# Serving the requests of a two-layer graph network while its second layer still runs: rows sorted by when they are ready, the output filled early, fewer sign passes in the sort

## The chip, the cores and the metric

The kernel runs on one core of a Trainium2 chip. The metric is the device time of one execution in microseconds, lower is better. The core has five engines that run their own programs and meet at semaphores: TensorE (PE), VectorE (DVE), ScalarE (ACT), GpSimd (POOL) and SyncE (SP). SP issues the plain transfers, POOL the indirect ones (a gather or a scatter by a list of row numbers, 128 rows each). All transfers run on the core's 16 DMA engines.

## What is computed

```python
NTOKEN, NINP, NHID, NEDGE = 18750, 64, 128, 300000
def gcn_conv(x, W, b, src, dst, n):
    h = x @ W
    deg = jnp.zeros((n,), h.dtype).at[dst].add(1.0) + 1.0
    dinv = jax.lax.rsqrt(deg)
    norm = dinv[src] * dinv[dst]
    agg = jax.ops.segment_sum(h[src] * norm[:, None], dst, num_segments=n)
    return agg + h * (dinv * dinv)[:, None] + b
h = gcn_conv(emb, W1, b1, src, dst, NTOKEN)
nodes = gcn_conv(h, W2, b2, src, dst, NTOKEN)
return nodes[input.reshape(-1)].reshape(512, 200, NINP)
```

`input` holds 102,400 request numbers from 23 to 149,996. A number past the last of the 18,750 rows is clamped to the last row, so about seven in eight requests take that one row. The output is 102,400 rows of 64 float32 numbers, 26.2 MB.

## The kernel before

Both weight matrices are multiplied into one ahead, so each layer is a sum over edges of scaled rows. The program has these stages.

1. Degrees of the nodes are counted with one-hot matmuls.
2. The 300,000 edges are sorted by a bitonic network on VectorE over 128 x 2560 keys (`steps`; `exchange` writes a minimum and a maximum, lines 1287 and 1288). The first seven levels work within a row of keys. Ahead of them `sign` steps multiply all keys by plus or minus one (line 1296), so that every exchange can go upward. Between levels PE turns the keys, and VectorE uses the time for `requests(n)`, one piece of work on the requests for each turn.
3. Two layers of 466 batches each (`NB`). In a batch PE gathers source rows out of the table in SBUF (line 989), ACT copies them out of PSUM (line 830), PE adds them into destination sums (line 1054), and VectorE makes the one-hot operands (lines 1465 and 1560). What does not fit this scheme (700 lists of 128 edges a layer) is fetched by POOL, row by row, from the table in HBM into `zring`, a ring of 18 buffers (line 684), and PE adds it (lines 1020 and 1025). The order of these items is a plan written ahead (`planned`, `ITEMS`). POOL waits on `zmm` for a free buffer, so it runs up to 18 items ahead of PE.
4. When a group of rows is complete (a unit, `UNITS`: three blocks of 128 rows, or two blocks of the last 33), VectorE scales it and SP stores it (`unit_out`). In layer one it goes to `table1`, in layer two to `nodes` (line 560), and all blocks of a group finish in the order of the groups.
5. The requests. Each partition owns 800 requests. VectorE has picked those that are not the last row, eight at a time with the largest keys first (`requests`, `comp`). The key holds the request's place in its upper bits and the row in its lower bits, so they are in the order of places. After layer two POOL gathers them, a column of 128 rows at a time (line 730), and scatters them into the output (line 739). It works by `q` of ten columns behind an `If`, as many as the fullest partition needs. Ahead of the scatters `filled` is awaited: SP has written the last row over the whole output (line 610), 25 rows a piece, from `zring`.

At the end VectorE turns `comp` into the two lists of numbers (lines 1573 to 1577) in the last batch. POOL's queue there, in program order: the last ring gathers, a skipped `If` for a slow way that is taken when lists overflow (`many`), three loads of counts, the wait for all stores of `nodes`, the gathers, the wait for `filled`, the scatters, the waits for their landing.

The fetch of sorted key rows that prepares layer one works in fifteen pieces (`prep_steps`): `rank_rows(g)` and `cell_rows(g)` on POOL stand between ring gathers, and `begins(g)` on VectorE waits for the first of them (line 1363). Piece 1 is fetched after the first 18 ring gathers, and `begins(1)` stands in batch 2.

## Time and profile before

| what | value |
|---|---|
| median of three executions | 4097.41 us (4090.86 to 4101.44) |
| the profiled execution | 4114.96 us, its span 4113.1 us |
| busy: PE, DVE, ACT, POOL | 2787.5, 3019.4, 1326.7, 1867.6 us |
| degrees and set-up | 0 to 363 us |
| sort | 363 to 1040 us |
| layer one | 1070 to 2433 us |
| layer two | 2433 to 3740 us |
| gathers and scatters of the requests | 3740 to 4113 us |

A busy share is an average over stages with different limits. The chain that ended last is the better guide: it is followed back from the last instruction, at each step to what released it.

### The profile page before, as it was taken

What the parts mean: (1) busy time and instruction counts of PE and PEld (TensorE: products, weight loads), DVE (VectorE), ACT (ScalarE), POOL (GpSimd) and SP (SyncE); (2) the same over time, 40 slices, a digit from 0 to 9 for tenths busy, and PEclk for the clock granted to TensorE, in tenths of its full rate; (3) what the DMA queues carried; (4) which work ended last, traced back from release to release, by engine and by line L of the source; (5) the groups of instructions that cost most, each with busy time, mean ns of one, the idle gap of its engine ahead of it and who ended that gap; (6) DMA issues with size and microseconds to landing.
All of it is one profiled execution on the core that took longest, in us unless ns stands there. A gap on an engine that the chain in (4) does not pass through costs nothing.

```text
span 4113.1 us, 74778 instructions
## 1 busy us (share of the span) xinstructions
PE 2787.5 (68%) x27730; PEld 2494.4 (61%) x27730; DVE 3019.4 (73%) x8656; ACT 1326.7 (32%) x3124; POOL 1867.6 (45%) x1717
## 2 busy tenths in 40 slices
PE   6996434421477888888888867888888888883000
PEld 5884222211367777877877766888887888882000
DVE  9999999999577887877777866777777777773000
ACT  5774212210433333433333322333333333331000
POOL 2000000000465556666656645666666565555765
PEclk9997566655699999999999988999999999996555
DMA  3000000000223233333333342333333333336400
GB/s 75 0 0 4 19 12 16 19 4 0 64 77 83 76 78 79 86 79 79 81 81 82 83 134 69 80 84 82 85 82 81 77 82 80 78 81 252 60 24 9
DMA packets 202648, 269.00 MB, mean 65 GB/s; under 512 B 99119, under 2 KB 111704, under 8 KB 202039
## 3 DMA queue, kind: packets, MB, share of 16 engines
q1 hardware_dynamic: 147912, 185.41, 15.1%
q0 software_dynamic: 54416, 79.31, 10.3%
q8 instruction: 203, 3.33, 0.3%
q14 instruction: 117, 0.96, 0.1%
HBM read 213.38 MB, written 52.14 MB: 65 GB/s over the span
## 4 chain that ended last, share of the span: by engine, by line
PE 47%; DVE 32%; issue 6%; another core or an unknown queue 6%; POOL 5%; ACT 2%; POOLq 1%; SPq 1%; DMA 0%; DVEq 0%; ACTq 0%
PE ps L989 17%; PE ps L1054 17%; PE ps L871 8%; DVE oh L1560 7%; DVE keys L1287 6%; DVE keys L1288 6%; DVE keys L1465 4%; POOL arena L730 3%; PE ps L1020 2%; POOL out L739 2%; DVE zoh L1544 2%; PE ps L937 1%; PE ps L1025 1%; POOLq L739 1%
## 5 line engine op out<-in xcount | busy, mean ns | idle before, releaser
L684 POOL DMA_INDIRECT zring<-table,sidx x1400 | 1560.2, 1114 | 1055.2 <-PE ps L1020 533.8
L989 PE MATMUL ps<-arena,keys 128*128 128x192 bf16 x11184 | 1283.9, 253 | 271.1 <-issue 132.1
L830 ACT ACTIVATE steps_oh<-ps 128x384 bf16<-128x384 f32 x1864 | 898.7, 490 | 1723.7 <-PE ps L989 1296.2
L1054 PE MATMUL ps<-steps_oh,oh 128*128 128x192 bf16 x11172 | 1276.9, 252 | 1.9 <-issue 1.9
L989 PEld LDWEIGHTS ps<-arena,keys 128*128 128x128 bf16 x11184 | 970.5, 100 | 340.1 <-issue 205.2
L1054 PEld LDWEIGHTS ps<-steps_oh,oh 128*128 128x128 bf16 x11172 | 985.7, 100 | 12.8 <-issue 3.1
L1560 DVE TENSOR_SCALAR oh<-io_h,dl 128x384 bf16<-128x384 int16 x3724 | 960.0, 319 | 44.9 <-remote 28.0
L1465 DVE TENSOR_SCALAR keys<-keys,lanes 128x1024 bf16<-128x1024 int16 x1398 | 596.5, 480 | 16.7 <-DMA keys<-srel 10.6
L639 POOL DMA_INDIRECT arena<-line,row_i x16 | 15.8, 988 | 1030.4 <-DVEq L1351 1025.9
L1544 DVE TENSOR_SCALAR zoh<-io_h,dl 128x128 bf16<-128x128 int16 x1172 | 261.2, 263 | 301.6 <-remote 147.5
L937 PE MATMUL ps<-ident,keys 128*128 128x128 f32 x464 | 100.1, 409 | 319.8 <-DVE keys L1288 315.3
L1020 PE MATMUL ps<-zring,zoh 128*128 128x192 bf16 x1172 | 217.7, 253 | 119.3 <-DVE oh L1560 79.7
L937 PEld LDWEIGHTS ps<-ident,keys 128*128 128x128 f32 x464 | 92.5, 222 | 335.6 <-DVE keys L1288 330.7
L1287 DVE TENSOR_TENSOR keys<-keys 128x1280 f32<-128x1280 f32 (+4 forms) x233 | 278.9, 1197 | 17.6 <-ACT keys L801 9.5
L1288 DVE TENSOR_TENSOR keys<-keys 128x1280 f32<-128x1280 f32 (+4 forms) x233 | 277.4, 1190 | 0.0
L758 ACT ACTIVATE steps_oh<-colf,arena 128x128 bf16<-128x128 f32 x784 | 240.4, 389 | 78.8 <-PE ps L871 78.7
L1138 DVE TENSOR_TENSOR oh<-iorep,arena 128x1024 bf16<-128x1024 bf16 (+1 forms) x392 | 258.6, 714 | 0.4 <-DVE arena L1188 0.4
L871 PE MATMUL ps<-oh 128*128 128x147 bf16 x1568 | 231.1, 314 | 0.3 <-DVE oh L1138 0.3
L1020 PEld LDWEIGHTS ps<-zring,zoh 128*128 128x128 bf16 x1172 | 99.2, 99 | 173.5 <-DVE oh L1560 119.2
L871 PEld LDWEIGHTS ps<-oh 128*128 128x128 bf16 x1568 | 173.2, 118 | 40.7 <-DVE oh L1138 17.6
L1547 DVE TENSOR_SCALAR ooh<-io_h,dl 128x384 bf16<-128x384 int16 x228 | 71.6, 324 | 161.2 <-PE ps L1054 89.6
L739 POOL DMA_INDIRECT out<-arena,oidx x130 | 127.7, 982 | 67.9 <-issue 67.9
(249 smaller groups left out, 1615.8 us busy)
## 6 DMA issues: line engine op xcount, KB each, us to landing
keys<-srel SPq DMA_DIRECT2D x466, 256.0 KB
out<-zring SPq DMA_DIRECT2D x1, 25600.0 KB
zring<-table,sidx POOLq DMA_INDIRECT x1400
table<-arena SPq DMA_DIRECT2D x19, 384.0 KB, 2.8
table<-sgn_l SPq DMA_DIRECT2D x38, 144.0 KB
nodes<-arena SPq DMA_DIRECT2D x38, 96.0 KB
arena<-in_L_rec_edge_index SPq DMA_DIRECT2D x2, 1171.5 KB, 6.6
arena<-nodes,oidx POOLq DMA_INDIRECT x130
```

What stands on the lines that cost most here:

```text
L684: pool.indirect_dma_start(out=zring[:, i % RING, :], out_offset=None, in_=rows_of, in_offset=bass.IndirectOffsetOnAxis(ap=sidx[:, col:col ...
L830: act.activation(grow[:, j % 2, h * 2 * ROW:(h + 1) * 2 * ROW], pg[h][:, 0:2 * ROW], ACT.Copy).then_inc(evac, 1)
L871: mm = pe.matmul(bank[:, 0:BLOCKS], lane[:, t // TT, :, t % TT] if steps is None else stp[:, t, :], blk[:, t // TT, :, t % TT], start=Fals ...
L989: mm = pe.matmul(pg[t // 2][:, t % 2 * ROW:(t % 2 + 1) * ROW], s_oh[:, j // 2 % 2, k, e:e + P], xtab[:, (w * WIN + k) * ROW:(w * WIN + k + ...
L1020: pe.matmul(pz[:, 0:ROW], zoh[:, u, :], zring[:, u, :], start=False, stop=(n == (ZT if blk < ZB - 1 else ZLAST) - 1)).then_inc(zmm, 1)
L1054: mm = pe.matmul(sums(sl, k), dwin[:, j % 2, t, k * P:(k + 1) * P], grow[:, j % 2, t * ROW:(t + 1) * ROW], start=False, stop=(w == CELLS - ...
L1138: dve.tensor_tensor(o.rearrange("p (s j t) -> p s j t", s=HH // TT, t=TT), iorep[:, 0:m, :].unsqueeze(1).to_broadcast([P, HH // TT, m, TT] ...
L1287: dve.tensor_tensor(b[:, :, 0, :], a[:, :, 0, :], a[:, :, 1, :], ALU.min).then_inc(k_stage, 1)
L1288: dve.tensor_tensor(b[:, :, 1, :], a[:, :, 0, :], a[:, :, 1, :], ALU.max).then_inc(k_stage, 1)
L1465: made = dve.tensor_scalar(s_oh[:, p % 2, k, :], srow[:, p % 2, :], lanes[:, k:k + 1], None, ALU.is_equal)
L1544: dve.tensor_scalar(zoh[:, place[item], :], io_h[:, 0:P], dl[:, col:col + 1], None, ALU.is_equal)
L1560: made = dve.tensor_scalar(dwin[:, j % 2, t, :], io_h[:, off:off + SUP * P], dl[:, c:c + 1], None, ALU.is_equal)
```

## The change

**Requests.** `nodes` gets a new layout (`stores`, `slot_of`): 38 slots of 512 rows, a group's three blocks and then one of the last 33 blocks. The key now holds 32767 minus the row's place in this layout in its upper bits and the request's place in its lower ten, so `comp` begins with the rows that are stored first. `requests(1)` has sixteen operations of 128x800 where it had three. The first 60 columns (`EG` = 6 times 10) get their lists in layer one (`places`, `early_checks`). In layer two POOL gathers them between ring gathers (`early_gather`), each ten once the units before `UPTO[q]` are stored. It scatters the first 20 (`SG` = 2) the same way (`early_scatter`). After layer two the `If` of a group that is done is skipped.

**Output.** The last block of the small lists comes first in layer two (`Z_ORDER`), so the last row is known early. SP reads it into `fill` as 128 x 16 copies and writes the output in 50 pieces, one after every second pair of batches. Layer two's first small list starts at batch 12 instead of 10.

**Sort.** Six of the seven sign steps are gone. The first six levels exchange upward and downward in four instructions ("two ways"), each half as wide.

**Fetch.** `rank_rows(1, 2)` stands before the first ring gather of layer one, and piece 1 begins in batch 5.

```diff
+SLOT = 4 * P
+EG, SG = 6, 2
+GROUPS = [groups_with((q + 1) * OG - 1) for q in range(EG)]
@@ steps of the sort
-        steps = [("sign", 0, k_b, k_a, 0, ALL, 0)]
+        steps = []
...
-            if 1 < k < 8:
+            if k == 7:
                 steps.append(("sign", k - 1, cur, other, done, ALL, 0))
...
+                if k < 7:
+                    steps.append(("two ways", (1 << bit, 1 << (k - 1 - bit)), cur, other, done, ALL, 0))
+                    done, cur, other = done + 4, other, cur
+                    continue
@@ vector: the step itself
+                elif what == "two ways":
+                    stride, n = k
+                    a, b = (x.rearrange("p (g d m t s) -> p g d m t s", d=2, m=n, t=2, s=stride) for x in (src, dst))
+                    for d in range(2):
+                        low, high = a[:, :, d, :, 0, :], a[:, :, d, :, 1, :]
+                        dve.tensor_tensor(b[:, :, d, :, d, :], low, high, ALU.min).then_inc(k_stage, 1)
+                        dve.tensor_tensor(b[:, :, d, :, 1 - d, :], low, high, ALU.max).then_inc(k_stage, 1)
@@ planned
+        Z_ORDER = [list(range(ZB)), [ZB - 1] + list(range(ZB - 1))]
-            total, given, items, wait_until = len(left) + OT, 0, [], 10 * layer
+            total, given, items, wait_until = len(left) + OT, 0, [], 12 * layer
+        UPTO = [units_for(q) for q in range(EG)]
+        STORED_AT = [UNITS[1][upto - 1][2] + 10 for upto in UPTO]
+        FILL_FROM, FILL_STEP, FILLS = 16, 2, RT // FILL
+        SCATTER_AT = 2 * (FILL_FROM + FILL_STEP * FILLS) + 16
         def prep_at(g):
-            return 2 + 4 * (g - 1)
+            return 2 + 4 * (g - 1) if g > 1 else 5
@@ sync: the fill
+            def fill_part(i):
+                if i == 0:
+                    for s in EMPTY:
+                        sp.dma_start(nodes[s * SLOT + SUP * P:(s + 1) * SLOT, :], acc3[:, BLOCKS, :]).then_inc(last_in, 16)
+                    sp.wait_ge(tab1_out[LAST_UNIT % UR], rows_out(LAST_UNIT + 1, LAST_UNIT % UR))
+                    sp.dma_start(fill.rearrange("p (t f) -> p t f", f=F),
+                                 nodes[LAST_AT:LAST_AT + 1, :].unsqueeze(1).to_broadcast([P, FILL, F])).then_inc(last_in, 16)
+                else:
+                    sp.wait_ge(last_in, 16 * (len(EMPTY) + 1))
+                    sp.dma_start(rows[:, i - 1, :], fill).then_inc(filled, 16)
@@ pool: in the loop over the items of layer two
+                    for q in range(EG):
+                        first = FIRST_ITEM[1][min(STORED_AT[q], NB)] + RING
+                        for n in range(OG):
+                            between.setdefault(min(first + 3 * n, NI), []).append((early_gather, q * OG + n))
+                    for t in range(SG * OG):
+                        between.setdefault(min(FIRST_ITEM[1][SCATTER_AT] + RING + 4 * t, NI), []).append((early_scatter, t))
@@ pool: after layer two
-                    with pool.If(most > r * ROUND + q * OG):
+                    with pool.If((again if q < EG else most) > r * ROUND + q * OG):
                         for t in range(q * OG, (q + 1) * OG):
                             pool.indirect_dma_start(
...
+                for q in [*range(SG, QG), *range(SG)]:
+                    with pool.If((again if q < SG else most) > r * ROUND + q * OG):
```

How the change moves instructions, at three places. First POOL from layer two to the slow way behind it, where `zring<-table,sidx` is a ring gather and the rows behind the COMPARE_AND_BRANCH are the skipped slow way; before:

```order
L684 DMA zring<-table,sidx 128x192 x700
L691 COMPARE_AND_BRANCH
L693 DMA keys<-line 128x20x128
L694 UNCONDITIONAL_BRANCH
L694 ISA
```

and now, around the third early group (item 477 of the ring gathers) and then from the end of the fifth (item 648 on), where `arena<-nodes,eidx` is an early request gather and `out<-arena,eidx` an early scatter:

```order
L798 DMA zring<-table,sidx 128x192 x4
L759 DMA out<-arena,eidx 102400x64
L798 DMA zring<-table,sidx 128x192 x11
L750 DMA arena<-nodes,eidx 128x64
L798 DMA zring<-table,sidx 128x192 x3
L750 DMA arena<-nodes,eidx 128x64
```

```order
L750 DMA arena<-nodes,eidx 128x64
L798 DMA zring<-table,sidx 128x192 x3
L750 DMA arena<-nodes,eidx 128x64
L798 DMA zring<-table,sidx 128x192 x25
L750 DMA arena<-nodes,eidx 128x64 x10
L808 COMPARE_AND_BRANCH
```

The early groups stand from ring item 261, 348, 477, 561 and 648 of 700 on, one gather after every third item. The sixth group has no item left and stands behind all of them. The 20 scatters stand from item 390 to 466, one after every fourth.

Second the SP queue in the first part of layer two, where `keys<-srel` feeds VectorE's one-hots, before:

```order
L569 DMA keys<-srel 128x1024 x10
L560 DMA nodes<-arena 128x3x64
L569 DMA keys<-srel 128x1024 x6
L560 DMA nodes<-arena 128x3x64
L569 DMA keys<-srel 128x1024 x2
```

and now, from the first stores on:

```order
L631 DMA nodes<-arena 128x3x64
L631 DMA nodes<-arena 128x64
L652 DMA keys<-srel 128x1024 x5
L640 DMA nodes<-arena 128x64 x5
L642 DMA res<-nodes 128x16x64
L652 DMA keys<-srel 128x1024
L631 DMA nodes<-arena 128x3x64
L652 DMA keys<-srel 128x1024
L646 DMA out<-res 128x1024
L652 DMA keys<-srel 128x1024 x2
L646 DMA out<-res 128x1024
```

Five small stores, the read of the last row and then 50 output pieces have come into the queue that feeds VectorE.

Third the first levels of the sort on VectorE, before:

```order
L1296 TENSOR_TENSOR keys<-keys,sgn_t 128x2560
L1287 TENSOR_TENSOR keys<-keys 128x1280
L1288 TENSOR_TENSOR keys<-keys 128x1280
L1296 TENSOR_TENSOR keys<-keys,sgn_t 128x2560
L1287 TENSOR_TENSOR keys<-keys 128x640x2
```

and now:

```order
L1453 TENSOR_TENSOR keys<-keys 128x640
L1454 TENSOR_TENSOR keys<-keys 128x640
L1453 TENSOR_TENSOR keys<-keys 128x640
L1454 TENSOR_TENSOR keys<-keys 128x640
L1453 TENSOR_TENSOR keys<-keys 128x320x2
```

The passes over all 2560 keys have gone, and each pair of instructions has become two pairs of half the width.

## Rows read from the trace of the kernel before

**Rows 1.** The page: its span, and the chain that ended last by line
```profile
span 4113.1 us, 74778 instructions
...
PE ps L989 17%; PE ps L1054 17%; PE ps L871 8%; DVE oh L1560 7%; DVE keys L1287 6%; DVE keys L1288 6%; DVE keys L1465 4%; POOL arena L730 3%; PE ps L1020 2%; POOL out L739 2%; DVE zoh L1544 2%; PE ps L937 1%; PE ps L1025 1%; POOLq L739 1%
```

**Rows 2.** Stretches: busy PE, PEld, DVE, ACT, POOL; PEclk, DMA share, GB/s
```profile
2500.00:3740.00 1240.00, 1067.08 (x11847) 999.61 (x11847) 914.26 (x3421) 436.33 (x906) 743.19 (x672) 0.95 0.32 79
3740.00:3902.00 162.00, 0.00 (x0) 0.00 (x0) 1.82 (x1) 0.00 (x0) 122.54 (x130) 0.50 0.63 187
3902.00:4113.10 211.10, 0.00 (x0) 0.00 (x0) 0.00 (x0) 0.00 (x0) 127.80 (x131) 0.50 0.09 17
```

**Rows 3.** The order of time on POOL: last table gather, first request gather
```profile
3709.05 0.94 POOL L684 DMA_INDIRECT zring<-table,sidx  x1 [1.15 <-PE ps L1020]
3740.15 0.94 POOL L730 DMA_INDIRECT arena<-nodes,oidx  x1 [30.16 <-issue]
```

**Rows 4.** The order of time, VectorE and the SP queue, end of layer two
```profile
3731.68 0.26 SPq L563 DMA_DIRECT2D nodes<-arena  x1
...
3734.15 1.03 DVE L1577 TENSOR_TENSOR dl<-keys 128x840 int32<-128x840 f32 x1
...
3736.90 0.38 SPq L560 DMA_DIRECT2D nodes<-arena  x1
```

**Rows 5.** The order of time on POOL: the stores of the requests
```profile
3902.41 1.03 POOL L739 DMA_INDIRECT out<-arena,oidx  x1 [0.30 <-issue]
...
3965.54 0.98 POOL L739 DMA_INDIRECT out<-arena,oidx  x1 [0.30 <-issue]
...
3987.30 0.98 POOL L739 DMA_INDIRECT out<-arena,oidx  x1 [4.62 <-issue]
...
4059.39 0.98 POOL L739 DMA_INDIRECT out<-arena,oidx  x1 [3.92 <-issue]
...
4096.71 0.98 POOL L739 DMA_INDIRECT out<-arena,oidx  x1 [0.31 <-issue]
```

**Rows 6.** Line 739: its steps in POOL's sequencer (POOLq) and on POOL
```profile
L739 POOLq MOVE  x130: 1/700/702, 3887.6 to 4081.0; - x130
```

**Rows 7.** Groups by line from 363 to 480 us, the sort's first levels
```profile
L1287 DVE TENSOR_TENSOR keys<-keys 128x1280 f32<-128x1280 f32 x25 | 37.3, 1492 | 0.9
...
L1296 DVE TENSOR_TENSOR keys<-keys,sgn_t 128x2560 f32<-128x2560 f32 x7 | 19.8, 2825 | 0.4 <-DVE onesf L1256 0.2
```

**Rows 8.** The order of time on VectorE: request steps between two sort levels
```profile
499.51 0.69 DVE L1287 TENSOR_TENSOR keys<-keys 128x512 f32<-128x512 f32 x1
...
500.72 0.57 DVE L1268 TENSOR_SCALAR dl<-io_r 128x800 int32<-128x800 int32 x1
...
501.93 0.99 DVE L1270 TENSOR_TENSOR dl<-dl,req 128x800 int32<-128x800 int32 x1
503.15 0.96 DVE L1287 TENSOR_TENSOR keys<-keys 128x768 f32<-128x768 f32 x1 [0.23 <-ACT keys L801]
```

**Rows 9.** The order of time at the start of layer one
```profile
1095.36 0.34 DVE L1363 TENSOR_SCALAR_CACHE_REDUCE k_e<-arena,lowest 128x128 f32<-128x128 f32 x1 [12.77 <-DMA arena<-line,row_i]
...
1101.17 0.49 ACT L830 ACTIVATE steps_oh<-ps 128x384 bf16<-128x384 f32 x1 [12.10 <-remote]
```

**Rows 10.** Groups by line from 2500 to 3700 us, layer two
```profile
L684 POOL DMA_INDIRECT zring<-table,sidx x667 | 738.7, 1107 | 462.4 <-PE ps L1020 253.6 <-issue 132.2 <-remote 48.1
...
L1465 DVE TENSOR_SCALAR keys<-keys,lanes 128x1024 bf16<-128x1024 int16 x657 | 279.7, 479 | 0.0
```

**Rows 11.** The chain that ended last, by line, 2500 to 3700 us
```profile
by line: PE ps L989 31.9%; PE ps L1054 31.7%; DVE oh L1560 8.2%; another core or an unknown queue 5.9%; issue 5.7%; PE ps L1020 4.1%; DVE keys L1465 3.1%; DVE zoh L1544 2.5%; PE ps L1025 2.2%; DVE arena L1471 1.3%; ACT steps_oh L830 1.3%; D
```

**Rows 12.** The same chain in order of time, start of layer two
```profile
2504.78 11.52 another core or an unknown queue
```

**Rows 13.** DMA from 3740 to 3902 us: the fill of the output
```profile
out<-zring SPq DMA_DIRECT2D x1, 25600.0 KB
```

**Rows 14.** DMA from 2500 to 3700 us, layer two
```profile
DMA packets 71350, 96.38 MB, mean 80 GB/s; under 512 B 32624, under 2 KB 32624, under 8 KB 71215
```

More of the change, by code:

```diff
@@ L1 @@
+import math
 from contextlib import ExitStack
@@ L23 @@
 RCOLS = -(-RT // ROUND) * ROUND
-FILL = 25
+FILL = 16
 BLOCKS = -(-NODES // P)
@@ L686, in _ @@
                         in_offset=bass.IndirectOffsetOnAxis(ap=sidx[:, col:col + 1], axis=0)).then_inc(gathered[i % RING], 16)
+                for what, g in between.get(NI, []):
+                    what(g)
                 if layer == 0:
@@ L1423, in prepare @@
                     rows_by_act(EARLY, GT, 2 * GT)
+                if j == LIST_AT - 6:
+                    places(comp[:, 0:EARLY_COLS], comp[:, 0:EARLY_COLS].bitcast(I32), eidx[:, :, :],
+                           src_of[:, 0:EARLY_COLS].bitcast(F32), beyond[:, 0:EARLY_COLS],
+                           [(q * OG, (q + 1) * OG, GROUPS[q] * SLOT) for q in range(EG)])
+                if j == LIST_AT - 5:
+                    early_checks()
                 if j == LIST_AT - 4:
```

212 lines of the change are left out of this document (154 added, 58 removed).

## The prediction

> **What bounds the kernel now.** I read the chain that ended last first, by line. PE and VectorE hold most of it, but two request lines of POOL stand there as well, L730 with 3% and L739 with 2% [rows 1]. The busy time by stretches says where: from 3740 us on PE, VectorE and ACT do nothing, and POOL alone works for 373 us [rows 2]. That is 9% of the span.
>
> The order of time on POOL splits this end. The first of 130 request gathers starts at 3740.15 us [rows 3], the first of 130 scatters at 3902.41, the last at 4096.71 [rows 5], and the span ends at 4113.1 [rows 1]. So a gather takes (3902.41 - 3740.15) / 130 = 1.248 us. The first 50 scatters take (3965.54 - 3902.41) / 49 = 1.288 us each. From the 61st at 3987.30 to the 101st at 4059.39 they take 1.80 us each, with one idle gap of about 4.6 us at the head of each ten. In this stretch the DMA engines have a share of 0.09 [rows 2], so it is not the transfer that is late but POOL's own program: its sequencer's step for a scatter has a median of 700 ns, and the first of them is done at 3887.6 us, 14.8 us ahead of the first scatter [rows 6]. This lead covers the first 50, then each ten waits for the sequencer.
>
> Ahead of the end lies layer two, 1240 us with PE busy for 1067 [rows 2]. Its chain is PE for some two thirds, and 11.6% of it is "another core or an unknown queue" and "issue", time that no instruction of the profile explains [rows 11]. POOL is no bound there: of 1200 us it works 738.7 and waits 462.4, most of it for a free ring buffer [rows 10]. The DMA share is 0.32 [rows 2].
>
> **The end, gathers.** 60 of the 130 gathers leave it in the program, but the sixth group stands behind the ring items. POOL is free from 3709.99 us [rows 3]; this group needs all units but the last. In the kernel before, the last unit but one is stored at 3731.68 us and the last at 3736.90 [rows 4], and the first gather follows that store by 3.25 us [rows 3]. With the same delay the sixth group starts at 3731.7 + 3.2 + 0.4 for a second store = 3735.3 us. Then 80 gathers run in a row: 80 x 1.248 = 99.8, and I add 1 us for the branches and count loads between them, since the sequencer runs ahead of POOL. The scatters start at 3836.1 instead of 3902.4: **-66.3 us**. The two more list operations on VectorE in the last batch (some 0.6 us each by the 0.57 us of [rows 8]) delay only the last unit, and the sixth group's 12.5 us cover that. Without this cover they would cost 1.3.
>
> **The end, scatters.** 110 stay. I expect the same course as before, 50 at 1.288, the slow pace up to the 100th column, the fast one behind it. Then 20 of the slow ones are gone, 20 x 1.80 = **-36 us**. At the fast pace alone it would be 20 x 1.288 = 25.8. If no slow stretch is left at all, the 110 take 141.7 instead of 194.3 + 1.3, so -54.
>
> **The fill.** One transfer of 25,600 KB goes [rows 13], and 50 of 512 KB come into layer two. It was hidden behind gathers, so nothing is won. There it adds 26.2 MB to the 96.4 MB of the 1200 us [rows 14], or 27% more. At the 187 GB/s of the stretch that held the old fill [rows 2] a piece takes at most 2.8 us, every 10.7 us (four batches of 1240 / 466 = 2.66 us). What hides it is that the lists for VectorE come two pairs of batches ahead: L1465 never sat idle in layer two, 0.0 us [rows 10]. Only the one read of the last row, 2048 pieces of 256 bytes, may be longer than this cover. If it ran at the pace of the gathers (1.25 us for each 128 of them) it would take 20 us and stop VectorE for about 20 - 10.7 = 9 us. I take 2.
>
> **Layer two, POOL.** 50 gathers and 20 scatters come in. Each takes 1.107 + 0.30 us there (the 0.30 is the gap between neighbours [rows 5, 10]), 99 us in all against 462 us of waiting. In an early group there are 4 DMAs for each 3 items. The 1.5 items a batch take 2.1 us now and 2.8 us then, against 2.66 us of batch time. Over 20 batches this falls behind by 3 us, and the ring's 18 items (12 batches) cover it. So POOL itself costs nothing. But the unexplained 11.6% is 139 us of 1200. I read it as time in which the engines wait for instructions or signals while POOL and the DMA engines are loaded. If it grows with the number of POOL's DMAs (70 on 667, 10%) it costs 14, if with the bytes (27%) 38, if with neither 0. I take 10. With the read above that is **+12 us**.
>
> A second start of the small lists, 10 and 11 items in batches 12 and 15 where 15 stood in batch 10, may soften a stop of 11.5 us at 2504.78 [rows 12]. Bounds 0 and -18; I take **-3**.
>
> **The sort.** Six passes of 2.825 us go [rows 7], with their 0.03 us gaps 17.1. In the first six levels 21 exchanges change from two instructions of 1280 to four of 640. The trace has 1280 columns in 1.492 us [rows 7], 768 in 0.96 and 512 in 0.69 [rows 8]. So 640 take 0.82. A pair overlaps by 0.08 (two of 1280 end 2.93 us after the first began), so an exchange goes from 2.93 to 3 x 0.74 + 0.82 + 0.03 = 3.07: 21 x 0.14 = +3. Two sign preparations become narrower, -0.5. The request keys have 16 operations instead of 3. Eleven of one input at 0.57 + 0.03 us and five of two inputs at 0.99 + 0.03 [rows 8] make 11.7 against 2.2. Only 0.23 us of waiting stand behind them [rows 8], so +9.3. Sum -17.1 + 3 - 0.5 + 9.3 = **-5 us**. If the new forms ran at twice these prices it would be +9 and more, which I hold as the upper end.
>
> **Layer one.** VectorE waited 12.77 us for the key rows of piece 1, up to 1095.36 us; now they are fetched ahead of the ring. But ACT stood still as well, for 12.10 us up to 1101.17, for nothing that VectorE gives [rows 9]. So most of the gain meets the next wait. Bounds 0 and -12.8; I take **-2**. The early lists and checks are some two dozen operations of 60 columns on VectorE, near 0.2 us each if they go by the shortest rows, in two batches: **+3**.
>
> **Sum.** -66.3 - 36 + 12 - 3 - 5 - 2 + 3 = -97.3 us. The span goes from 4113.1 to 4015.8, and the profiled execution from 4114.96 to 4017.7. The median lies 17.6 lower than that execution, so I forecast 4097.4 - 97.3 = **4000 us**.
>
> **Rivals.**
> - *Everything gives.* Layer two absorbs all (0 instead of +12), the stops at the starts of both layers go (-18 and -12.8), and no slow stretch is left in the scatters (-54): -66.3 - 54 - 18 - 5 - 12.8 + 3 = -153, 3944 us. For it: POOL and the DMA engines have room. Against it: slow scatters need a reason to go away, and none is in the change.
> - *The layer pays for the bytes.* The unexplained time grows by 38 and the read of the last row stops VectorE for 9: 35 us more than my 12, 4035 us. For it: a DMA share that rises from 0.32 to some 0.4 in the stretch of the fill.
> - *The end loses in its branches.* The gaps of 4.6 us stand where an `If` begins, and now 14 are skipped. At 4.6 us each 64 us come back, 4064. Against it: before, the group of columns 130 to 139 was skipped too, between the last gather and the scatter at 3902.41, and POOL's gap there is the usual 0.30 [rows 5]. The Trainium skill, Runtime: NRT & Kernel Launch, section Instruction fetch mechanics, says that a taken branch to a page not held stops the engine for a fetch. That speaks against the change. The one skip in the trace shows no stop, but it had the sequencer's lead of 14.8 us to hide in, and I keep the case for that.
> - *Slower than before.* The place is the SP queue of layer two. A list for VectorE now stands behind stores, the row's read and a fill piece. If a piece held it beyond its cover of 10.7 us, every second pair would stop. The price is 50 times the excess, and from an excess of 2 us on each piece (12.7 instead of at most 2.8 for transfer) the 97 us are lost. At 2.3 us it gives 4115. Against it: 0.0 us of idle time before L1465 now, and pieces of a fifth of the cover.
> - *No effect.* The early checks find a row that is not yet stored, or the flag sends everything to the slow way, or POOL stops at each early group as long as it saves: within 12 us of 4097, or far above.
>
> **How the numbers follow.** My forecast with its own range 3965 to 4025 has 0.66, everything gives 0.12, the bytes 0.11, the branches 0.05, slower 0.035, no effect 0.025. The range 3950 to 4045 takes in half of the first rival and all of the bytes; some 0.16 stays outside. 0.3% is 12 us, about what a measurement of this kernel can tell from none. Faster by more: 0.94; within: 0.025; slower: 0.035.
>
> **What would show it.** The last instructions of PE should stand near the same time as before (within 15 us), the first tail gather of the sixth group about 5 us before the last store's landing, 80 gathers at 1.25 us, then 110 scatters, some of them with gaps near 4.6 us. The sign line should have one row of 2.8 us, the exchanges of 640 columns 0.82 us. L1465 should keep an idle time of almost nothing. I am wrong if layer two is longer by over 40 us, if the fill pieces land late, or if scatters in the end take 1.8 us throughout.

## The result, and the profile after

The change makes the kernel slower. It takes 4133.95 us (median of 6 runs, 4119.71 to 4139.3) against 4098.34 us (median of 6, 4090.86 to 4111.49): a ratio of 1.0084, 95% interval 1.0067 to 1.0102. The profiled execution took 4134.77 us, and its span is 19.8 us longer than that of [rows 1]. I had forecast 4000 us, so the time moved the other way.

The page of the changed kernel first: the span, and the chain that ended last, by engine and by line (L1125 and L1190 were L989 and L1054, L1749 was L1560, L1654 was L1465, L798 was L684).

```profile
span 4132.9 us, 74982 instructions
...
PE 44%; DVE 33%; another core or an unknown queue 8%; issue 5%; POOL 4%; ACT 2%; DMA 1%; POOLq 1%; SPq 1%; DVEq 0%; ACTq 0%
PE ps L1125 16%; PE ps L1190 15%; PE ps L1007 8%; DVE oh L1749 8%; DVE keys L1438 6%; DVE keys L1439 5%; DVE keys L1654 4%; DVE zoh L1733 2%; PE ps L1156 2%; POOL out L875 2%; POOL arena L862 2%; ACT steps_oh L966 1%; PE ps L1161 1%; PE ps L1073 1%
```

The request lines (L875, L862) hold 2% each where L730 had 3% and L739 2% [rows 1]. "Another core or an unknown queue", time that no instruction of the profile explains, is 8%. The stretches of [rows 2], with the same columns:

```profile
2500.00:3740.00 1240.00, 1000.62 (x10717) 924.90 (x10717) 821.55 (x3079) 394.30 (x818) 745.20 (x678) 0.91 0.36 96
3740.00:3902.00 162.00, 95.63 (x1065) 88.90 (x1065) 85.19 (x316) 39.92 (x83) 92.52 (x91) 0.83 0.23 55
3902.00:4132.90 230.90, 0.00 (x0) 0.00 (x0) 0.00 (x0) 0.00 (x0) 151.09 (x156) 0.50 0.19 18
```

In the 1240 us in which PE issued 11,847 matmuls before it issues 10,717 now. The layer is not done at 3740 us. Its last one-hot (L1749) starts at 3850.7 us; before it was 3731.1.

POOL in order of time, from the last ring gather on. The bracket is the idle time ahead of the row:

```profile
3828.91 0.95 POOL L798 DMA_INDIRECT zring<-table,sidx  x1 [0.64 <-PE ps L1156]
3854.11 1.10 POOL L750 DMA_INDIRECT arena<-nodes,eidx  x1 [24.25 <-issue]
...
3871.24 0.94 POOL L862 DMA_INDIRECT arena<-nodes,oidx  x1 [4.28 <-issue]
```

These rows answer to [rows 3]. The sixth group of early gathers starts 3.4 us behind the last one-hot, so 70 of the 80 early DMAs stand inside the layer and ten behind it. The 70 late gathers follow after a gap of 4.28 us, and the first scatter starts at 3958.78. Cut at the same points, the two executions compare so:

| stretch | before | after | difference | forecast |
|---|---|---|---|---|
| up to the first ring gather of layer two | 2436.4 | 2421.1 | -15.3 | -4 |
| from there to the last one-hot | 1294.7 | 1429.6 | **+134.9** | +9 |
| last one-hot to first late scatter | 171.3 | 108.1 | -63.2 | -66.3 |
| first late scatter to the end | 210.7 | 174.1 | -36.6 | -36 |
| sum | 4113.1 | 4132.9 | +19.8 | -97.3 |

So the end came out as worked out, and layer two took back more than all of it. Over the second stretch alone, from the first ring gather to the last one-hot, the windows rows before and after are:

```profile
2436.40:3731.10 1294.70, 1102.27 (x12187) 1032.10 (x12188) 937.59 (x3514) 448.07 (x930) 772.84 (x700) 0.94 0.34 84
2421.10:3850.70 1429.60, 1136.80 (x12187) 1050.82 (x12188) 937.04 (x3513) 448.44 (x930) 841.68 (x770) 0.91 0.36 97
```

PE does the same 12,187 matmuls. It is idle for 100 us more, and busy for 35 us more: the granted clock falls from a mean of 0.94 to 0.91, since it stands at its lower level (0.5, which is 1.2 GHz) for 258 us of the stretch where it was 149. A matmul takes 0.37 us at that level and 0.25 at the full one. Ahead of every one of these falls PE had been idle, mostly in one of the stops described below, so the lower clock is counted as a part of what the idle time costs.

One piece of this is plain in the trace. SyncE's queue (SPq), then VectorE:

```profile
2539.44 0.43 SPq L642 DMA_DIRECT2D res<-nodes  x1
2541.07 8.07 SPq L652 DMA_DIRECT2D keys<-srel  x1
```

```profile
2571.11 1.28 DVE L1654 TENSOR_SCALAR keys<-keys,lanes 128x1024 bf16<-128x1024 int16 x3 [21.46 <-DMA keys<-srel]
```

The read of the last row, 2048 pieces of 256 bytes of one and the same row, goes out at 2539.44 us, and a list for VectorE (L652) goes out 1.6 us behind it in the same queue. VectorE runs dry 8.6 us later, at 2549.65. The DMA view of 2541 to 2566 us shows what moved:

```profile
DMA packets 1894, 0.49 MB, mean 19 GB/s; under 512 B 1893, under 2 KB 1893, under 8 KB 1894
```

Next to nothing but the row read moves, at 19 GB/s, and at that pace its 524 KB take some 27 us. The DMA engines have a share of only 0.07 in this view, so they are not what is busy. The list lands after it, and VectorE stops for 21.46 us. More than 100 us are left, and no single wait has them. Above all ACT stands still more: here between 2600 and 3200 us (waited for, total, times, longest), first before, then after.

```profile
ACT steps_oh L830 <- PE ps L989: 296.8, 331, 2.6
ACT steps_oh L830 <- remote: 56.0, 23, 5.3
```

```profile
ACT steps_oh L966 <- PE ps L1125: 287.6, 305, 2.6
ACT steps_oh L966 <- remote: 88.5, 28, 6.7
```

The rows with "remote" are stops of ACT, PE and VectorE together. They begin about every 38 us, 28 activations (14 batches) apart, in both kernels. From 2500 us on I count 21 gaps of ACT above 2.6 us before and 39 after, often two in a row now.

### The profile page after: what moved, and what is told of

Its sections match the earlier page's. It is cut to its first block, busy times and chain, and to the rows that moved or that the text cites. A ratio compares the mean times of both kernels' runs of the same rounds, so it can differ in the third digit from the quotient of the medians.

```text
span 4132.9 us, 74982 instructions
## 1 busy us (share of the span) xinstructions
PE 2826.0 (68%) x27730; PEld 2519.0 (61%) x27730; DVE 3014.6 (73%) x8729; ACT 1329.7 (32%) x3124; POOL 1857.8 (45%) x1711
## 3 DMA queue, kind: packets, MB, share of 16 engines
q1 hardware_dynamic: 153976, 186.08, 15.3%
## 4 chain that ended last, share of the span: by engine, by line
PE 44%; DVE 33%; another core or an unknown queue 8%; issue 5%; POOL 4%; ACT 2%; DMA 1%; POOLq 1%; SPq 1%; DVEq 0%; ACTq 0%
PE ps L1125 16%; PE ps L1190 15%; PE ps L1007 8%; DVE oh L1749 8%; DVE keys L1438 6%; DVE keys L1439 5%; DVE keys L1654 4%; DVE zoh L1733 2%; PE ps L1156 2%; POOL out L875 2%; POOL arena L862 2%; ACT steps_oh L966 1%; PE ps L1161 1%; PE ps L1073 1%
## 5 line engine op out<-in xcount | busy, mean ns | idle before, releaser
L798 POOL DMA_INDIRECT zring<-table,sidx x1400 | 1545.0, 1104 | 1091.7 <-PE ps L1156 557.6
L1125 PE MATMUL ps<-arena,keys 128*128 128x192 bf16 x11184 | 1298.9, 255 | 333.9 <-issue 150.8
L1190 PE MATMUL ps<-steps_oh,oh 128*128 128x192 bf16 x11172 | 1290.1, 253 | 2.6 <-issue 2.5
L1125 PEld LDWEIGHTS ps<-arena,keys 128*128 128x128 bf16 x11184 | 979.6, 101 | 412.9 <-issue 219.0
L1190 PEld LDWEIGHTS ps<-steps_oh,oh 128*128 128x128 bf16 x11172 | 996.8, 101 | 15.0 <-issue 3.7
L1749 DVE TENSOR_SCALAR oh<-io_h,dl 128x384 bf16<-128x384 int16 x3724 | 959.5, 319 | 46.6 <-PE ps L1190 22.9
L1654 DVE TENSOR_SCALAR keys<-keys,lanes 128x1024 bf16<-128x1024 int16 x1398 | 596.2, 481 | 34.2 <-DMA keys<-srel 28.6
L1438 DVE TENSOR_TENSOR keys<-keys 128x1280 f32<-128x1280 f32 (+4 forms) x212 | 247.6, 1168 | 16.5 <-ACT keys L937 9.4
L1439 DVE TENSOR_TENSOR keys<-keys 128x1280 f32<-128x1280 f32 (+4 forms) x212 | 246.3, 1162 | 0.0
L937 ACT ACTIVATE keys<-ps 128x512 f32<-128x512 f32 x70 | 41.5, 598 | 310.6 <-PE ps L1073 310.4
```

The lines of the kernel that those rows point to most:

```text
L798: pool.indirect_dma_start(out=zring[:, i % RING, :], out_offset=None, in_=rows_of, in_offset=bass.IndirectOffsetOnAxis(ap=sidx[:, col:col ...
L1125: mm = pe.matmul(pg[t // 2][:, t % 2 * ROW:(t % 2 + 1) * ROW], s_oh[:, j // 2 % 2, k, e:e + P], xtab[:, (w * WIN + k) * ROW:(w * WIN + k + ...
L1190: mm = pe.matmul(sums(sl, k), dwin[:, j % 2, t, k * P:(k + 1) * P], grow[:, j % 2, t * ROW:(t + 1) * ROW], start=False, stop=(w == CELLS - ...
L1438: dve.tensor_tensor(b[:, :, 0, :], a[:, :, 0, :], a[:, :, 1, :], ALU.min).then_inc(k_stage, 1)
L1439: dve.tensor_tensor(b[:, :, 1, :], a[:, :, 0, :], a[:, :, 1, :], ALU.max).then_inc(k_stage, 1)
L1654: made = dve.tensor_scalar(s_oh[:, p % 2, k, :], srow[:, p % 2, :], lanes[:, k:k + 1], None, ALU.is_equal)
```

## The experiments

The runs fell on different chips. The kernel before took 4137 us on the chip of e1 to e4 and 3637 to 3639 us on those of all other runs, so ratios are compared, and absolute times only within one kind of chip. The first kind, with the stops shown above, is called a chip with stops, the second one without. The comparison itself (4098 us) ran on a chip with stops whose time agrees with neither. Sixty batches are thirty pairs of batches, and where an expectation says thirty batches it means the pairs.

| run | what | ratio to before | interval |
|---|---|---|---|
| e1 | POOL's early DMAs behind the layer | 1.0128 | 1.0111 to 1.0145 |
| e2 | fill behind the layer, no early scatters | 1.0119 | 1.0102 to 1.0135 |
| e3 | both, row read mended | 1.0080 | 1.0061 to 1.0099 |
| e4 | row read mended | 1.0044 | 1.0031 to 1.0058 |
| e5 | e4, early DMAs spread to one in eight | 0.9981 | 0.9963 to 0.9998 |
| e7, g2 | sort and fetch alone | 0.9961, 0.9964 | 0.9947 to 0.9975, 0.9953 to 0.9975 |
| e9 | the change, on the other kind of chip | 1.0039 | 1.0026 to 1.0051 |
| e10 | sort, fetch, 20 gathers behind the ring | 0.9994 | 0.9984 to 1.0003 |
| e11, f2, g1 | before with 60 more DMAs on POOL | 1.0162, 1.0117, 1.0152 | 1.0145 to 1.0179, 1.0091 to 1.0142, 1.0135 to 1.0169 |
| f1 | e7 with the new order of ring items | 0.9991 | 0.9982 to 1.0001 |

e6, e8, e12, f3 and f4 were executed once each, for their profiles: 3656.68, 3639.29, 3635.69, 3654.22 and 3638.24 us. In these and in all single profiles below a few us can be chance: the same layer takes 1061 to 1065 us in three profiles of the kernel before.

**e1, POOL's early work out of the layer.**

```diff
-  between.setdefault(min(first + 3 * n, NI), []).append((early_gather, ...))
+  between.setdefault(NI, []).append((early_gather, ...))
-  between.setdefault(min(FIRST_ITEM[1][SCATTER_AT] + RING + 4 * t, NI), []).append((early_scatter, t))
+  between.setdefault(NI, []).append((early_scatter, t))
```

> The changed kernel with its 60 early gathers and 20 early scatters issued behind the last ring item of layer two instead of between the items; the 50 fill pieces and the row read stay in the layer. The last one-hot of layer two (L1749) started at 3850.7 us in the changed kernel and at 3731.1 before. Theory P (POOL's extra DMAs slow the layer, more than one microsecond each): the layer ends some 75 us earlier, near 3775, and the end pays about 60 x 1.25 + 20 x 1.5 = 105 us back, so about 4165 us. Theory F (the bytes and packets of the fill pieces do it) or L (new row layout, split stores and their waits, other order of the ring items): the layer still ends near 3850 and the time is about 4240 us.

Measured: 4192.4 us beside 4136.9, a ratio of 1.0128. Against the 4098 us for which they were written, the expectations were 1.016 (P) and 1.035 (F, L), so P is nearest. The last one-hot starts at 3875.9, not at 3775: the layer has a new stop of 48 us in its last batches, which is read under e3. Ahead of it the pace can be read cleanly. From 2650 to 3650 us POOL issues, in e1 and then in e4 (same chip, same fill pieces, the DMAs of the requests in the layer; the row read, which e4 has mended, lies ahead of this stretch):

```profile
L798 POOL DMA_INDIRECT zring<-table,sidx x527 | 604.0, 1146 | 396.8 <-PE ps L1156 213.2 <-issue 104.0 <-remote 54.3
```

```profile
L801 POOL DMA_INDIRECT zring<-table,sidx x493 | 548.7, 1113 | 370.0 <-PE ps L1159 175.2 <-issue 95.1 <-remote 66.3
L753 POOL DMA_INDIRECT arena<-nodes,eidx x40 | 43.3, 1084 | 12.2 <-issue 12.2
L762 POOL DMA_INDIRECT out<-arena,eidx x20 | 21.3, 1065 | 6.1 <-issue 6.1
```

60 request DMAs in the stretch push out 34 ring items. At 527 items in 1000 us these are 64.5 us, or **1.08 us for each DMA**, although POOL idles 397 us in the one and 388 in the other. The same 360 batches (from the 90th to the 630th list operation of the layer) take 1029.9 us in e1 and 1102.5 in e4 with the same 60 DMAs among them, which makes it 1.21. That is theory P, with a price of 1.1 to 1.2 us.

**e2, the fill pieces out of the layer.**

```diff
-EG, SG = 6, 2
+EG, SG = 6, 0
-  if layer and p >= FILL_FROM and (p - FILL_FROM) % FILL_STEP == 0:
-      fill_part((p - FILL_FROM) // FILL_STEP)
+  if layer and p == FILL_FROM:
+      fill_part(0)
...
+  for i in range(1, FILLS + 1):     # behind the layer
+      fill_part(i)
```

> The changed kernel with the 50 fill pieces issued after layer two, as the old fill was, and no early scatters (they need the fill); early gathers and the broadcast read of the last row stay in the layer. Theory F: the layer ends 40 us earlier or more, near 3805. Theory P: of the extra DMAs only the 20 scatters are gone, so the layer ends 15 to 25 us earlier, near 3830. Theory L: no change, 3850. The total is worse in any case, since 137 us of fill now lie behind the layer with only 70 gathers (88 us) for cover: about 4134 + 50 + 36 less what the layer gives, 4180 to 4220.

Measured: 507 ring items and 40 early gathers in the same 1000 us, so the gathers alone push out 20 items (0.95 us each). Sixty batches in the fill's time take 172, 178 and 185 us; in e4, with the pieces among them, 174, 179 and 186. From 2700 to 3000 us 76 and 122 GB/s are moved. Theory F falls. The last one-hot starts at 3857.5 us, though, where P had 3830; the expectations were written for the faster chip of the comparison.

**e3, nothing of the requests in the layer.** The two edits above together, and the row read of e4.

> Nothing of the request work is left between the ring items of layer two: 60 gathers behind the last item, no early scatters, fill pieces behind the layer, and the last row read once for each partition (128 pieces) and copied to 16 columns by a second DMA. What stays of the change: sort in two ways, early key rows, keys by row slot, node rows in the new layout with their split stores and waits, and the early lists. Theories P and F: the layer takes what it took before, and the time is that of before less 5 to 15 us, 4085 to 4093. Theory L: the layer stays long by most of its 120 us, and the time is over 4150 us.

Measured: 1.0080, not the 0.997 to 0.999 of theories P and F. It has 527 ring items in the 1000 us, as many as e1, and its 360 batches take 1030.5 us where e1's took 1029.9: the 50 fill pieces, which e1 has and e3 has not, cost nothing that shows. Most of the surprise stands at the layer's end. ACT, in order of time, and then POOL, which issues the 60 gathers in this stretch:

```profile
3788.75 0.49 ACT L971 ACTIVATE steps_oh<-ps 128x384 bf16<-128x384 f32 x1 [4.45 <-remote]
3805.05 0.49 ACT L971 ACTIVATE steps_oh<-ps 128x384 bf16<-128x384 f32 x1 [15.81 <-remote]
3837.22 0.49 ACT L971 ACTIVATE steps_oh<-ps 128x384 bf16<-128x384 f32 x1 [31.68 <-remote]
```

```profile
3833.44 0.94 POOL L755 DMA_INDIRECT arena<-nodes,eidx  x1 [0.30 <-issue]
3834.69 0.94 POOL L755 DMA_INDIRECT arena<-nodes,eidx  x1 [0.30 <-issue]
3856.80 1.12 POOL L755 DMA_INDIRECT arena<-nodes,eidx  x1 [21.16 <-issue]
```

PE's matmuls for this activation were done at 3806.7. ACT goes on at 3837.22, 1.6 us after POOL's run of 50 gathers has ended (3834.69 + 0.94). In e1 the run ends at 3859.4, and ACT, which stood for 31.68 us as well, goes on at 3859.07. From this I made theory B: a stop lasts until POOL pauses. In the middle of the layer the traces leave it open. Of the gaps of ACT above 2.6 us without a visible releaser, 16 of 17 in the kernel before end within 4 us after the start of a pause of POOL, and 23 of 37 in the changed one, and a moment picked at random does so in some 60 of 100 cases. With pauses above 1 us alone the gaps keep nearly these shares, and the random moment has only some 45 of 100. But a PE that stands frees no ring buffers, and that makes POOL pause too, so such a count cannot tell which causes which.

**e4, the row read mended.**

```diff
     if i == 0:
-        sp.dma_start(fill, nodes[LAST_AT:LAST_AT + 1, :].unsqueeze(1).to_broadcast([P, FILL, F]))
+        sp.dma_start(fill[:, 0:F], nodes[LAST_AT:LAST_AT + 1, :].to_broadcast([P, F]))
+    elif i == 1:
+        ...                               # waits for the read
+        sp.dma_start(fill[:, F:], fill[:, 0:F].unsqueeze(1).to_broadcast([P, FILL - 1, F]))
```

> The changed kernel, but the last row is read once for each partition (128 pieces of 256 bytes instead of 2048 of the same row), and a second DMA, four batches later, copies it inside SBUF to the 16 columns; all fill pieces are four batches later. Theory R (the read of one row 2048 times runs at 20 GB/s and holds the lists behind it in the queue): the stop of 21.5 us of VectorE at 2571 is gone and the time falls by about 20 us, to 4114. Rival: the engines would have waited for ring rows or instructions in the same stretch anyway: under 8 us are won.

Measured: the stop is gone, and the ratio is 1.0044 where the change had 1.0084 on its own chip: theory R holds, with about 16 us (7 to 25 by the two intervals, on two chips). The DMA view of e4 from 2564.6 to 2572 us, with the second DMA, narrows down what was slow:

```profile
DMA packets 2282, 1.07 MB, mean 144 GB/s; under 512 B 2037, under 2 KB 2037, under 8 KB 2282
...
res<-res SPq DMA_DIRECT2D x1, 480.0 KB
```

Its 1920 pieces of 256 bytes are nearly as many as the old read's 2048, now out of SBUF, and they are through within this view of 7.4 us, beside two lists. So it is not the number of pieces, but where they are read from: HBM, and there one and the same row. Which of these two it is was not tested.

**e5, the early DMAs spread.**

```diff
-  between.setdefault(min(first + 3 * n, NI), [])
+  between.setdefault(min(first + 8 * n, NI), [])      # scatters: 8 * t for 4 * t
```

> The kernel with the mended row read (e4) in which the early gathers stand every eight ring items instead of every three, and the early scatters every eight instead of every four. Theory B (a stop of VectorE, ACT and PE, which begins about every 38 us, lasts until POOL has worked off what it has to issue and pauses; at four DMAs for three items POOL has 2.8 us of work for a batch of 2.66 us and never pauses): with 1.5 x 1.125 x 1.35 = 2.3 us a batch POOL pauses again, the stops fall back from 5 to 8 us to 3 to 5, and the layer is 25 to 50 us shorter than in e4 (ratio to the kernel before 0.992 to 0.998 instead of 1.0044). Rival C (each extra DMA costs the layer a fixed time wherever it stands, some 1 us): no change from e4, 1.004.

**e6, the gathers behind the layer wait for its end.** On top of e3:

```diff
+  if layer:
+      for n in range(UR): pool.wait_ge(tab1_out[n], rows_out(NU, n))
   for what, g in between.get(NI, []):
```

> e3 (no request work in the layer) with a wait of POOL for the last store of layer two before the 60 gathers behind the ring items. In e3 ACT stood still from 3789.2 to 3837.2 us (15.8 and 31.7 us) while POOL issued these gathers back to back, and went on 1.6 us after the last of them. Theory B: without the run of gathers the stop is gone, and the last batches of the layer (L1659 from the 630th list operation to the last) take some 122 us as in the kernel before, not 171. Rival D (something else of the changed kernel stops ACT there): 171 us again.

**e7, sort and fetch alone**: the diff's hunks on the sort's steps and signs, the early fetch of the key rows, nothing else.

> The kernel before with two parts of the change alone: the first six merge levels sorted in two ways without sign passes, and the key rows of piece 1 fetched ahead of the ring. By my terms of the forecast the sort gives 17.1 - 3 + 0.5 = 14 us here (the request keys, which cost 9, are not in this kernel), and the fetch 0 to 13: the time is 14 to 27 us below that of before, ratio 0.9935 to 0.9966. Rival: layer one is bound by something behind it (ACT's stop), the sort's gain stays alone at most 10 us, or the layers take it back: ratio 0.998 or more.

**e8, the kernel before.**

> The kernel before, unchanged, for its profile on the same chip as the others. If this chip is slower in layer two by itself, the thirty batches between the 90th and the 630th list operation take over 165 us here as in e3 (168 to 189); if they take 155 to 170 as in the profile before, then e3's longer layer comes from the parts of the change that stay in it (theory L: row layout, stores, order of items, place of the code).

Measured, all on a chip that I had not reckoned with: the kernel before takes 3638.65 us. Sixty batches take 133 us, and from 2300 us on ACT has no gap above 2.6 us in the layer. So e6 could not test its theory (there was no stop to remove), and neither could e5. e6 takes 3656.68 us, and its layer two, with no DMA of the requests, no fill piece and the mended read in it, takes 1075.9 us from the first ring gather to the last one-hot, 13 more than the 1062.9 of e8 on the same chip. e5 still tells something. It gained 4.5 us on before, where the change itself lost 16 in e9. But this layer takes 1157.2 us in e5 and 1178.5 and 1167.0 in e9 and f3, and the row read alone accounts for 24 to 28 of that (sixty batches around it take 136 us in e5 and in e6, 164 and 160 in e9 and f3). Spreading won nothing here: on a chip without stops a DMA on POOL costs as much at one in eight as at one in three, as rival C says.

The two views that say why, on the chips without stops, from 2700 to 3200 us: first the windows row (busy time as in [rows 2]), then PE's waits, of the kernel before (e12) and of the change (e9).

```profile
2700.00:3200.00 500.00, 496.27 (x5916) 485.33 (x5914) 452.97 (x1703) 221.47 (x451) 396.37 (x341) 1.00 0.42 99
...
PE ps L1020 <- DVE oh L1560: 1.7, 8, 0.3
```

```profile
2700.00:3200.00 500.00, 452.48 (x5223) 432.94 (x5220) 402.37 (x1512) 195.95 (x399) 395.38 (x344) 0.99 0.42 102
...
PE ps L1156 <- DMA zring<-table,sidx: 32.4, 35, 2.5
```

POOL has 341 DMAs in one and 344 in the other, and its busy time with 0.30 us of gap for each fills the 500 us in both (396.37 + 341 x 0.30 = 498.7). Each of the 341 gaps is 0.30 us, so it is at its limit already in the kernel before, with 1.46 us for each DMA. In the change 48 of the 344 are requests. That leaves 296 ring items, 13% fewer, and PE's matmuls fall by 12%. Ring rows come late, and PE waits for them: 32.4 us where it waited for none.

**e9, e10, e11, e12.** The change on this kind of chip; the version that seemed best; and the price of POOL's DMAs by itself, with this edit of the kernel before:

```diff
+  if layer and i >= 270 and (i - 270) % 7 == 0 and (i - 270) // 7 < 60:
+      pool.wait_ge(extra_in, 16 * ((i - 270) // 7))
+      pool.indirect_dma_start(out=extra[:, :], out_offset=None, in_=rows_of, ...).then_inc(extra_in, 16)
```

> The changed kernel, unchanged, so that the others of this call can be set against it on one chip. If this is a chip on which the layers have stops of all engines every 38 us (kernel before near 4100 us), theory B expects 1.008 as in the first comparison. If it is one without stops (kernel before near 3640 us, where e5 was 0.998), POOL issues without a pause in layer two of the kernel before, at 1.45 us a DMA, and the 80 extra DMAs cost some 80 x 1.45 = 116 us less what the ring has in store, and the row read some 20: with 66 + 26 + 14 us won elsewhere the time is within 30 us of before, ratio 0.995 to 1.008.

> The version that the runs so far point to. Sort, early key rows and the sorted requests stay; nothing of the request work stands between the ring items; two groups (20 gathers, 25 us) are issued behind the last ring item, where POOL waited 30.2 us for the last stores; fill behind the layer under the other 110 gathers, row read mended. Theory: 25 us from the gathers and 5 from the sort, less some 12 that e6's layer was longer than that of before: 15 to 25 us below before, ratio 0.993 to 0.996. Rival: on a chip with stops, the run of 20 gathers holds a stop of ACT for up to 25 us at the layer's end, and nothing is won: 1.000 or more.

> The kernel before with 60 more indirect DMAs on POOL in layer two and nothing else: after every seventh ring item from the 270th on, a second gather of the same rows into a tile that nobody reads. This leaves the result as it is and measures the price of POOL's extra DMAs by itself. Theory P: POOL has no room in this layer, each costs its own 1.45 us: +60 to +87 us, ratio 1.016 to 1.024. The forecast's reading (POOL has 462 us of waiting in 1200): 0 to +8 us, ratio 1.000 to 1.002.

> The kernel before, unchanged, for its profile on the chip of this call: whether its layer two has stops (thirty pairs of batches take 155 to 172 us) or none (133 us).

Measured: e11 +57.6 us, that is 0.96 us a DMA. From 2700 to 3200 us, its windows row and its waits:

```profile
2700.00:3200.00 500.00, 472.48 (x5542) 454.66 (x5540) 428.37 (x1599) 207.71 (x423) 392.12 (x355) 1.00 0.42 97
...
PE ps L1029 <- DMA zring<-table,sidx: 22.3, 26, 2.5
...
POOL extra L691 <- issue: 13.4, 44, 0.3
```

The reading of the forecast (0 to 8 us) is refuted by measurement, and theory P's 1.45 us is too much as well. POOL got 355 DMAs into the 500 us here, 1.41 us each, while VectorE was busy for 428 us instead of 453; this is a part of the difference, the rest is not explained. e9 has 1.0039. e10 has 0.9994, nothing won over before, and misses its 0.993 to 0.996. Its 20 gathers run from 3285 to 3314 us, but the layer is 16 us longer (1077.0 against 1061.0), its last one-hot starts at 3299.9 instead of 3284.6, and the pause behind the last ring item was only 24 us here (3269.1 to 3293.3), not 30.

**f1 to f4, g1, g2.** f1 takes e7 and adds the other order of the ring items alone; the rest are repeats.

```diff
-  left = [("z", blk, n) for blk in range(ZB) ...];  wait_until = 10 * layer
+  left = [("z", blk, n) for blk in Z_ORDER[layer] ...];  wait_until = 12 * layer
```

> The kernel with the sort and the fetch (e7, ratio 0.9961) plus the changed order of the ring items of layer two: the last block's rows first, the second block of the small lists from batch 12 on instead of 10. Nothing of the requests is changed. If this order makes layer two some 10 us longer, as it was in e6 and e10, the ratio is 0.998 to 1.000. If it does nothing, 0.995 to 0.997, and the longer layer of e6 and e10 comes from the stores of the new row layout or the early lists.

> The kernel before with 60 extra DMAs, as in e11 (where +57.6 us, 0.96 us each, was measured). On a chip with stops, theory B (a stop lasts until POOL pauses, so its extra work comes back as longer stops) expects again +50 to +90 us, ratio 1.012 to 1.022; the forecast's reading (POOL's waiting swallows them) 0 to +8 us. On a chip without stops: +50 to +65 us again.

> The changed kernel, for its profile on the chip of this call: layer two from the first list to the last 120 us longer than in f4 on a chip with stops, about 110 us on one without.

> The kernel before, for its profile on the chip of this call: sixty batches take 155 to 172 us where there are stops, 133 to 138 us where there are none.

> The kernel before with 60 extra DMAs of POOL in layer two, a third time. On a chip with stops theory B expects +50 to +90 us (ratio 1.012 to 1.022), the forecast's reading 0 to +8 us (up to 1.002). On a chip without stops +42 to +58 us, as in e11 and f2.

> Sort and fetch alone, again. Where there are no stops 0.9961 was measured (14 us). If the gain is VectorE's alone it is 14 us on a chip with stops too, 0.9966; if layer one's stop of ACT goes with it up to 13 us more, 0.9935.

Measured: the order of items costs 11 us by the ratios (0.9991 against 0.9961; 5 to 17 by the intervals), 4.5 of them visible in the layer's length (1070.4 against 1066.0 us), 3 ahead of it, where the order cannot be the cause. The sixty DMAs cost 42.7 us in f2, less than the 50 expected, and 55.3 in g1, with e11 a mean of 52 us or 0.86 each. Sort and fetch alone repeat at 0.9964. None of these runs fell on a chip with stops, so the price of a dummy DMA was not measured there.

## Why the prediction was wrong

**The step that failed** stands under "Layer two, POOL": "So POOL itself costs nothing." I set 99 us of new work against 462 us of waiting [rows 10], and put down 10 us for all side effects. Measured, a DMA more in this layer costs 1.08 to 1.21 us on a chip with stops (e1 against e4) and 0.71 to 0.96 us on chips without (f2, g1, e11), so the 70 that stand in it cost 75 to 85 us on the first kind and 50 to 67 on the second. Two things were wrong in the reading. Each of the 667 gaps holds the 0.30 us between neighbours, 200 us in all, which belong to the price of a DMA and are no room. And I divided POOL's work by the mean batch of 2.66 us. That mean holds the stops. Without them a batch takes 2.22 us, and POOL needs 1.5 x 1.46 = 2.19 of it: between two stops it has next to no room. That POOL is the limit is shown where there are no stops, by POOL's gaps, all of 0.30 us, and by PE's waits for ring rows (e9, e11). Where there are stops the price is shown, the reason for it argued.

The account for the comparison's own chip, with prices from other chips: +134.9 us in the layer, of which 21.5 are the stop behind the row read, 75 to 85 are 70 DMAs of POOL, and 13 are what e6 keeps of the change (5 to 11 of it perhaps the other order of the ring items, f1). Some 15 to 25 us stay open; e3 points the same way (527 ring items in 1000 us with no request DMA, where the kernel before has 555, though on another chip).

On chips without stops the account of layer two closes to within 17 us. From the first ring gather to the last one-hot it takes 1061.0 us in e12 and 1178.5 in e9 (+117.5), 1065.3 in f4 and 1167.0 in f3 (+101.7). The row read is 164 - 136 = 28 or 160 - 136 = 24, what e6 keeps is 13, and 70 DMAs at 0.86 are 60: 101 and 97 us. With e11's 0.96 they are 67, and the sums 108 and 104.

**The read of the last row.** The mechanism was named, the size not: I took 2 us, with 9 for the bad case. It was 21.5 us, since the read took some 27 us and not 20, VectorE had 8.6 us of cover and not 10.7 from the list's issue on, and the list's own landing came on top. That the lists come two pairs of batches ahead covers a list that lands at once, not one that stands behind such a read.

**The bytes** ("the layer pays for the bytes"): no. e1 and e3 keep the same pace with and without them, and so do e4 and e2 in the fill's time.

**The slow rival** had the right end and the wrong place. No fill piece held a list: behind the row read L1654 never waits for one again. The forecast that came nearest in time was this one, at 0.035, and not for its reason.

**The end.** Right: -63.2 for -66.3 and -36.6 for -36. The slow scatters stayed, their sequencer step is again 700 ns. The course was not quite the forecast one: 60 fast ones come first instead of 50, and four gaps of 3.25 to 4.62 us are left of six. At the skipped branches stands one gap of 4.28 us, ahead of the 70 gathers, and none ahead of the scatters; that is not 64 us. The Trainium skill, Runtime: NRT & Kernel Launch, section Instruction fetch mechanics, says that a taken branch to a page not held stops the engine for a fetch. More than that one gap of such stops does not show here.

**The sort.** Right, and larger. The last exchange of 512 columns starts at 1013.70 us after 1021.65, -8.0 for the -5. Without the new request keys it starts at 1004.96 in e7 against 1022.34 in e8, and at 1004.38 in f1 against 1021.12 in f4, so the two-way sort gives 17 (I had 14). In f3, with the keys, it starts at 1014.23, so the keys cost near 10 (I had 9.3).

**The fetch.** The early fetch takes away VectorE's wait for piece 1. On chips without stops the next piece's wait takes its place, 16.69 us in e7 against 17.27 in e8, and nothing is won. On the comparison's chip VectorE does not wait for key rows any more, ACT's stop of 12.10 us [rows 9] is one of 11.67 up to 1093.38 us, and layer one, between the first ring gathers of the two layers, is 7.3 us shorter (1359.0 for 1366.3), where my terms made it 1 us longer. With the sort's 8.0 these are the 15.3 us of the table. That the fetch gives the 7.3 is not shown; a stop more or less would do it.

**The start of layer two.** ACT's stops of 10.3 and 8.6 us, ending at 2500.4 and 2509.4, stand where 7.3 and 11.6 stood, the second of them that of [rows 12]. Nothing was won.

The best version is the smallest, e7: sort and fetch alone, 0.9961 and 0.9964. It beats both kernels on the chips without stops; on one with stops it was not run.

## What to carry to other kernels

Before work is moved onto an engine that "waits 40% of the time", divide its work by the pace between the stalls, not by the mean pace, and count its fixed gaps as work. Moving DMAs from an idle end into a layer pays only if their engine has room there. Here a gather saves 1.25 us at the end and costs about one in the layer, and the rest of the change (a read, an order of items) decides the sign. And test the price with a dummy: one run that adds 60 idle copies told more than all rearrangements of the real ones.

## What the runs showed of the hardware

- One kernel takes 3637 to 3639 us on four chips, 4137 on the chip of e1 to e4 and 4098 in the comparison, with nearly the same busy times up to 1000 us. The difference is the stops in both layers, with the lower granted clock behind them (0.94 over layer two against 1.00 from 2700 to 3200 us in e12), and the slow scatters at the end. The scatter's step in POOL's sequencer has a median of 29 ns on the one kind and 700 ns on the other, first in e12, then in the changed kernel of the first comparison:

```profile
L739 POOLq MOVE  x130: 29/29/29, 3440.9 to 3606.2; - x130
```

```profile
L875 POOLq MOVE  x110: 1/700/709, 3944.7 to 4104.2; - x110
```

- On the chips with 29 ns no scatter is slow: 130 of them take 166 us (3455.7 to 3622.0), 1.29 each. So the 1.80 us of [rows 5] and the change's -36 belong to the chip; on the others it is -26 (178.2 to 152.4 us from the first scatter to the end).
- A gather keeps POOL for 0.945 us at the end, where VectorE is idle, and for 1.17 and 1.15 us on average in the layer (e12 and e9, 2700 to 3200 us), where VectorE is busy 91% and 80% of the time. The Trainium skill, SBUF — State Buffer, section SBUF: two separate sides, says that POOL, which writes the descriptors of its DMAs itself, is locked out of a port that it shares with VectorE while VectorE runs certain fast operations. The rows agree with that but do not show the lock.
- 2048 reads of one row of 256 bytes go at 19 GB/s with a DMA share of 0.07, where the old fill went at 187 [rows 2] and 1920 pieces of 256 bytes out of SBUF were through within 7.4 us (e4). In e4 128 such reads delayed nothing that I could find: no list is waited for behind them.
- What holds ACT, PE and VectorE in a stop stays open. The two longest, 31.68 us each, ended within 1.6 us of the end of a run of 50 DMAs of POOL (e1, e3). For the short ones POOL's pauses can be cause or result, and no experiment removed POOL's run on a chip that has stops.
